# First expert rows asked for inside the attention block, and two batches routed earlier

## The reference, cut to what matters

```python
x = x + _L0_xattn_ref(_layernorm(x, axis=-1), ctx_2048, ctx_2048, ...)   # 16 heads of 8 per batch
x = x + _L0_ffn_ref(_layernorm(x, axis=-1), gate_w, w13, w2)             # 64 experts, 8 chosen per token
# _L0_ffn_ref
logits = jnp.einsum('th,eh->te', x, gate_w)
topk_w, topk_idx = jax.lax.top_k(jax.nn.softmax(logits, axis=-1), 8)
h = jax.nn.silu(x @ w13_e[:128].T) * (x @ w13_e[128:].T)                 # for each expert e
out += c[:, None] * (h @ w2_e.T)
```

## Time and profile before

| | |
|---|---|
| median of 3 executions | 681.9 us |
| the profiled execution's own time | 680.48 us |
| its span, first to last instruction | 678.0 us |
| attention block | 64.6 to 262.7 us |
| first expert stage (held_phase) | 270.9 to about 420 us |
| busy: PE, DVE, ACT, POOL | 481.2, 362.2, 260.7, 368.8 us |
| mean granted TensorE clock | 0.839 |

### The profile page before, as it was taken

One profiled execution on the slowest core, in us unless ns is written; L12 is line 12 of the kernel. 1 busy time (PEld: TensorE's weight loads), 2 busy tenths in 40 slices (PEclk: granted clock), 3 DMA queues, 4 the chain that ended last, 5 costly groups with the idle time before them and its releaser, 6 DMA issues.

```text
span 678.0 us, 12350 instructions
## 1 busy us (share of the span) xinstructions
PE 481.2 (71%) x3519; PEld 368.3 (54%) x3520; DVE 362.2 (53%) x1105; ACT 260.7 (38%) x621; POOL 368.8 (54%) x517
## 2 busy tenths in 40 slices
PE   2641898788888430699989996176674599999960
PEld 1530344344443210588878874165453599999950
DVE  6981675799985560145444443565744144444426
ACT  0351065566668210333323331133342355555520
POOL 9494311116666673156555556226666787777730
PEclk9785597899989655699999999566886699999985
DMA  5089989856579696789999733959922333333327
GB/s 187 0 204 232 338 308 281 236 105 186 169 248 281 205 406 280 218 250 329 327 311 323 264 118 111 390 217 338 401 74 88 94 106 103 106 97 95 128 63 288
DMA packets 78131, 144.15 MB, mean 213 GB/s; under 512 B 12639, under 2 KB 56687, under 8 KB 76289
## 3 DMA queue, kind: packets, MB, share of 16 engines
q1 hardware_dynamic: 52048, 86.41, 39.5%
q0 software_dynamic: 13968, 32.29, 13.0%
q10 hardware_dynamic: 12064, 24.84, 12.5%
HBM read 85.14 MB, written 66.78 MB: 224 GB/s over the span
## 4 chain that ended last, share of the span: by engine, by line
PE 33%; DMA 12%; DVE 5%; POOL 5%; issue 2%; ACT 1%; SPq 1%; POOLq 0%; DVEq 0%
PE sc_ps L1814 11%; DMA hd_side<-held 6%; PE hd_ps_up L1252 6%; PE sc_ps L1796 5%; DMA rows<-hd_side_out,hd_side_target 3%; PE hd_ps_out L1258 2%; DMA sc_rows<-rows 2%; PE hd_ps_x L1230 2%; PE sc_ps L1804 1%; POOL sc_n_root L1494 1%; PE sc_ps L1749 1%; PE sc_ps L1761 1%; POOL sc_n_full L1492 1%; POOL listed L688 1%; PE sc_ps L618 1%
## 5 line engine op out<-in xcount | busy, mean ns | idle before, releaser
L1027 DVE TENSOR_REDUCE at_top<-at_ps_top 128x2 f32<-128x512 f32 x128 | 83.0, 685 | 42.9 <-PE at_ps_top L932 41.8
L1399 POOL DMA_INDIRECT rows<-hd_out,hd_rows x64 | 62.2, 972 | 57.4 <-DVE hd_out L1350 37.6
L1099 ACT ACTIVATE at_prob<-at_ps_score 128x512 f32<-128x512 f32 x128 | 72.3, 594 | 47.8 <-PE at_ps_score L950 47.4
L1252 PE MATMUL hd_ps_up<-hd_x_turned,e_arena 128*128 128x160 f32 x512 | 82.9, 306 | 0.0
L1814 PEld LDWEIGHTS sc_ps<-sc_t_turned,sc_up_w 128*112 128x112 f32 x672 | 81.2, 181 | 2.6
L1814 PE MATMUL sc_ps<-sc_t_turned,sc_up_w 128*112 128x128 f32 x672 | 82.4, 277 | 0.0
L932 PE MATMUL at_ps_top<-e_arena 96*128 96x256 bf16 x256 | 55.4, 304 | 37.0 <-PEq L107 21.9
L1252 PEld LDWEIGHTS hd_ps_up<-hd_x_turned,e_arena 128*128 128x128 f32 x512 | 76.4, 193 | 8.7 <-issue 6.2
L688 POOL DMA_INDIRECT held<-e_extended,e_address x64 | 62.3, 973 | 25.4 <-issue 17.7
L1387 DVE TENSOR_TENSOR hd_inner<-hd_silu,hd_ps_up 128x160 f32<-128x160 f32 x64 | 20.6, 322 | 83.4 <-ACT hd_silu L1337 83.4
L1709 POOL DMA_INDIRECT listed<-sc_empty,sc_index x48 | 46.7, 974 | 14.6 <-issue 12.8
(11 more groups left out here) (267 smaller groups left out, 941.1 us busy)
## 6 DMA issues: line engine op xcount, KB each, us to landing
e_arena<-in_weights SPq DMA_DIRECT2D x52, 384.0 KB, 11.3
held<-e_empty ACTq DMA_DIRECT2D x16, 960.0 KB, 6.3
hd_rows<-held SPq DMA_DIRECT2D x15, 768.0 KB, 9.9
e_w<-in_weights SPq DMA_DIRECT2D x16, 704.0 KB, 10.1
sc_rows<-rows SPq DMA_DIRECT2D x8, 1024.0 KB, 7.3
sc_tile_rows<-listed SPq DMA_DIRECT2D x42, 144.0 KB, 2.2
parts<-op_parts SPq DMA_DIRECT2D x8, 576.0 KB, 6.4
e_arena<-in_weights ACTq DMA_DIRECT2D x12, 384.0 KB, 4.2
```

The source lines that it names most:

```text
L1027: nc.vector.reduce_max(top[:, 2 * h:2 * h + 2], ps_top[at % TOPS][:], AX_X).then_inc(top_found, 1)
L1099: nc.scalar.activation(prob[at % RING][:], ps_score[at % SCORES][:], ACT.Exp, scale=scale).then_inc(prob_ready, 1)
L1252: op = nc.tensor.matmul(ps_up[e % 2][:, part, :], w[:, k, part * P:(part + 1) * P], x_turned[g % 2][:, j, k, :], start=k == 0, stop=k == 1)
L1399: nc.gpsimd.indirect_dma_start(rows_out, to, out_ap, None, bounds_check=TOKENS * LAYER0.chosen - 1, oob_is_err=False).then_inc(semaphore, 16)
```

## The change: what it does

Two buffers, rows0 and side0, which stood in held_phase as the first of its two rings, are allocated in Held, outside the attention's space, together with the five semaphores of their first loads. The five loads of group 0 are issued at the end of attend_phase's SP list, behind a wait for `scattered`; held_phase's SP list begins with group 1. The routing table gets a set of offsets for batch 4, and another for batch 5: all pieces from norm or turn on come up to 8 steps earlier. Batch 3's scatters are again split into four and four, 8 steps apart, so that its last four alternate with the first of batch 4 (in the order 3.4, 4.0, 3.5, 4.1, 3.6, 4.2, 3.7, 4.3, batch and number). merge(5) waits for rank_read too.

```diff
 class Held:
+        self.rows0 = s.sbuf("rows0", [P, EACH, ROW0], F32)
+        self.side0 = s.sbuf("side0", [P, ROW0], F32)
+        self.first_loaded = [s.sem(f"first_loaded{j}") for j in range(EACH)]
+        self.side0_loaded = s.sem("side0_loaded")
+
+    def load_first_rows(self, sp):
+        sp.wait_ge(self.scattered, 16 * LAYER0.chosen * B)
+        for j in range(EACH):
+            if j == 1:
+                sp.dma_start(self.side0[:], self.of_expert[0:EACH, P * ROW0:].rearrange("e (r n) -> e r n", n=ROW0))\
+                    .then_inc(self.side0_loaded, 16)
+            sp.dma_start(self.rows0[:, j, :], self.of_expert[j, 0:P * ROW0].rearrange("(r n) -> r n", n=ROW0)).then_inc(self.first_loaded[j], 16)
...
 class RoutingSteps:
-    LAST_BUT_TWO = dict(AMID, turn=45, keep=46, score=49, choose=49, expo=50, targets=50, rank=50, places=51, weights=51, scatter=53)
+    LAST_BUT_THREE = dict(AMID, turn=45, keep=46, score=49, choose=49, expo=51, rank=51, places=52, targets=53, weights=54, scatter=54)
+    LAST_BUT_TWO = dict(AMID, norm=40, turn=43, keep=44, score=47, choose=47, expo=48, rank=48, places=49, targets=49, weights=50, scatter=51)
...
-        of_batch = [self.AMID] * (B - 3) + [self.LAST_BUT_TWO] + [self.LAST_TWO] * 2
+        of_batch = [self.AMID] * (B - 4) + [self.LAST_BUT_THREE, self.LAST_BUT_TWO] + [self.LAST_TWO] * 2
...
-            apart = H // 2 if first < B * H - H - 4 else LAYER0.chosen // 2
+            apart = H // 2 if b < B - 4 else LAYER0.chosen // 2
...
 attend_phase, sync:
                 ring.load(sp, e)
+            held.load_first_rows(sp)
...
 attend_phase, tensor:
-                if b >= B - 2:
+                if b >= B - 3:
                     pe.wait_ge(routing.rank_read, b)
...
-                    if b + 1 < B - 2:
+                    if b + 1 < B - 3:
                         pe.wait_ge(x_ready, b + 2)
...
 held_phase:
-        rows = [s.sbuf(f"rows{n}", [P, EACH, ROW0], F32) for n in range(RING)]
-        side = [s.sbuf(f"side{n}", [P, ROW0], F32) for n in range(RING)]
+        rows = [held.rows0] + [s.sbuf(f"rows{n}", [P, EACH, ROW0], F32) for n in range(1, RING)]
+        side = [held.side0] + [s.sbuf(f"side{n}", [P, ROW0], F32) for n in range(1, RING)]
...
-            sp.wait_ge(held.scattered, 16 * LAYER0.chosen * B)
-            for g in range(RING):
+            for g in range(1, RING):
                 load_rows(g)
```

More of the change, by code:

```diff
@@ L1141, in held_phase @@
         rows_loaded = [s.sem(f"rows_loaded{n}") for n in range(RING)]
-        first_loaded = [s.sem(f"first_loaded{j}") for j in range(EACH)]
-        side_loaded = [s.sem(f"side_loaded{n}") for n in range(RING)]
+        first_loaded = held.first_loaded
+        side_loaded = [held.side0_loaded] + [s.sem(f"side_loaded{n}") for n in range(1, RING)]
         stored = [s.sem(f"stored{n}") for n in range(OUTS)]
@@ L1175, in load_rows @@
                 n = g % RING
-                if g == 0:
-                    for j in range(EACH):
-                        if j == 1:
-                            sp.dma_start(side[n][:], of_expert[0:EACH, P:HELD, :]).then_inc(side_loaded[n], 16)
-                        sp.dma_start(rows[n][:, j, :], of_expert[j, 0:P, :]).then_inc(first_loaded[j], 16)
-                    return
                 sp.dma_start(rows[n][:], of_expert[EACH * g:EACH * (g + 1), 0:P, :].rearrange("e p n -> p e n"))\
```

## The result

| | kernel before | changed kernel |
|---|---|---|
| median, us (15 runs each, in turn on one chip) | 681.49 | 677.17 |
| ratio, 95% interval | 1 | 0.9937 (0.9911 to 0.9962) |
| the profiled execution: time, span, us | 680.48, 678.0 | 675.59, 673.1 |

The change makes the kernel 4.3 us faster (681.49 - 677.17), by the interval 2.6 to 6.1. The forecast was 675.8 inside 672.8 to 681.2.

What follows compares the result with a forecast made beforehand. The chain of waits was taken to count from PE's start in the expert stage, held back by POOL's scatters and the block's end. Routing 2.0 plus early loads 4.1, 6.1 us, took the median of 681.9 to 675.8, range 672.8 to 681.2.

Steps and rivals of the forecast that it cites:

- Batch 4's steps: Attention's routing: batch 4's weights at 215.55 instead of 221.34, scatter 4.0 at 216.7, with waits at merge(5) and norm(5).
- POOL's end: End of attention: POOL's 35 scatters from 216.7 end at 260.7 instead of 262.66, 2.0 us sooner.
- The tightest batch: Attention's routing: batch 7 wanted at 250.85, ready at 249.5 to 250.3, so no wait, by half a microsecond.
- Group 0's loads: End of attention: `scattered` full 4.0 us after POOL's last scatter, side tile issued at 265.2, landing 5.94 us later at 271.1.
- The block's end: Attention's end: SP there at 267.3, POOL at 267.1, new block 1.9 us on at 269.2.
- The rival that put the price behind the last arrival: Block's end: POOL's 6.4 us begin once SP has come; PE gains 0.7 us, time 681.2; chance 0.14.
- that of the stretched issues: Block's end: SP's five loads meet full queues, take 7.5 us, PE starts 4.3 us later, time 686.2; chance 0.08.
- PE's start: Start of the expert stage: PE starts at 271.15 instead of 277.30, 6.1 us sooner, released by the side tile.
- Group 1 and on: Expert stage: group 1's loads go at 269.2, slack falls from 3.3 to 1.3 us and holds; ring moves as a whole.
- the rival: Expert stage: transfers set the ring's pace or group 1 is late, 3 us of 6.1 return, time 678.8; chance 0.10.
- The sum: Whole kernel: routing 2.0 and group 0 asked for early 4.1, 6.1 us in all, giving 675.8.

Runs made afterwards that it cites:

- side in four: Changed kernel with group 0's four row loads issued by ACT and its side tile by SP as four loads of 32 rows; ratio to kernel before 0.9925.
- rows on ACT: Changed kernel with SP asking for group 0's side tile alone and ACT for its four row tiles; ratio to kernel before 0.9941.
- Batch 3 earlier too: Changed kernel with batch 3's steps also moved earlier and its first four scatters six heads earlier; ratio to kernel before 0.9919.
- 15 copies behind the last: Changed kernel with 15 small unread copies on POOL behind its last scatter, ahead of the block's end; ratio to kernel before 0.9948.
- 28 copies, first run: Changed kernel with 28 small unread copies on POOL ahead of scatter 4.0; ratio to kernel before 0.9945, repeated 1.0004.
- the buffers alone: Kernel before with only group 0's two buffers and five semaphores moved to Held, loads still in the expert block; ratio to kernel before 1.0009.

## Why the prediction was right, by its own steps

*Batch 4's steps.* Foretold: 4.0 at 216.7, 5.8 us sooner. In distances from the cut it went from 15.96 (222.47 - 206.51) to 10.09 (218.22 - 208.13): 5.9 sooner. The wait ahead of it is 0.66 us and not about 1.5, since 3.0 itself came later (3.10 us after the cut and not 2.58): ACT's weights of batch 3 hold it for 1.03 us. The waits at merge(5) and norm(5) are there.

*POOL's end.* Foretold 2.0 us sooner; the pair of traces gives 1.7, the means over four and six traces 1.4, pairs of like clock 1.1 to 1.6, the time 1.5 (0.2 to 2.9). So this term was too large by 0.3 to 0.9 us. The sum took one pair of landmarks where the distance varies from run to run by more than the term. Most of the variation goes with the clock, though side in four has a short stretch (54.82) at 0.86. In the first 20 us behind the cut the mean granted clock was 1.00 of full (2.4 GHz) in the changed kernel's trace and 0.84, a mix of its two levels, in that of rows on ACT:

```profile
208.10:228.10 20.00, 15.55 (x160) 7.22 (x160) 10.19 (x40) 14.36 (x34) 14.41 (x20) 1.00 0.78 252
```

```profile
208.60:228.60 20.00, 17.09 (x146) 7.66 (x144) 7.62 (x33) 13.61 (x32) 13.40 (x19) 0.84 0.78 244
```

*The tightest batch.* Foretold: batch 7 ready half a microsecond ahead of its scatter. In the trace of the changed kernel its weights end at 250.39, 42.26 us from the cut, and it is sent at 44.27. In that with the slower clock its address is ready at 45.1, and POOL waits:

```profile
254.14 0.95 POOL L701 DMA_INDIRECT held<-e_extended,e_address  x1 [0.45 <-DVE e_address L693]
```

So this step held by 2 us at full clock and failed by 0.45 us below it. Batch 3 earlier too shows it as the next bound even at full clock.

*Group 0's loads.* The landing 3.95 us behind the last scatter (266.54 - 262.59) was foretold as 4.0, and SP issues 0.02 us after it and not 0.16. I had argued that the late weights in the queue cost at most 0.5 us. They do not delay the side load, as the trace showed; that they delay the last scatter's landing, by 2.3 us, I had taken into the 4.0 without seeing it. The side tile took 5.41 us for 5.94.

*The block's end.* Foretold: POOL 6.4 us behind its last scatter, SP 6.6, then 1.9. Measured: SP 6.43 (269.02 - 262.59), then 1.58, and 8.01 in all. The rival that put the price behind the last arrival would have had 8.27 behind SP's fifth issue; it is refuted by 1.58 here. That of the stretched issues is refuted too: five in 2.46 us. The DRAIN records show the race: with no loads of SP's ahead of it POOL arrives 6.45 to 6.88 us after its last scatter (three traces), and SP, with its five issues, 6.60 after it. In the five traces with all five issues on SP and no copies POOL's record ends 0.01 to 0.02 us behind SP's, so close that it may end by SP's arrival and not by POOL's own work: SP is last or level with POOL. It costs next to nothing either way, since the block begins 7.68 to 8.06 us behind the last scatter in these five and 7.83 to 8.27 in the three without the issues. Where the weights run on longest (rows on ACT, side in four) POOL needs 7.41 and 7.50, where they have landed 5.3. From the end of POOL's record to the new block it is 1.38 to 1.40 us and not 1.9, and in the trace of the kernel before POOL took 6.88 and not 6.4: the prediction had the sum from the trace (8.27) and the split wrong by half a microsecond, which did no harm here.

*PE's start.* Foretold 6.1 us sooner. From the cut it is 64.25 us (272.38 - 208.13) where it was 70.79 (277.30 - 206.51): 6.5. The margin behind it is thin: PE could have run from about 271.56 (block at 270.60 and 0.96), 0.8 us ahead of the side tile.

*Group 1 and on.* No wait of PE for group 1 in the changed kernel's trace, and the expert stage kept its length there. With the block 3 us late (15 copies behind the last) the chain does run through group 1's side load (278.30 for 8.27 us), so the slack was real and about as small as foretold. In two more traces PE waits for group 1, 0.74 us (28 copies, first run) and 0.29 (side in four). And the stage did not keep its length in every trace: from PE's start to the `sc_rows` load it is 146.8 to 147.3 us in the three traces that ask late and 146.8 to 150.8 in the eleven that ask early, 148.2 on the mean. A microsecond given back there isn't shown, with so few late traces, but it isn't excluded either; the rival had put it at 3.

*The sum.* 6.1 us foretold; the means of both measurements are 4.3 and 6.2 under the kernel before, by the two ratios together 5.0, and against the buffers alone it is 5.8 (4.1 to 7.6). The early ask is 4.2 of it (foretold 4.1), the routing 1.5 (foretold 2.0). In the traces the early ask brings more than foretold (4.4 to 4.9 us from POOL's last scatter to PE's start), above all since the side tile took 5.4 and not 5.94 us, and the routing less: that PE's start came out so near is in part two misses that cancel. Between that start, 6.5 us sooner, and the 5.0 in the time lie the scatter between runs and perhaps the microsecond in the expert stage; the record doesn't tell them apart.

## What to carry to other kernels

A load at the head of a new block pays the old block's end even when its data has long landed; asking for it as the last piece of the old block, into a buffer that both blocks own, takes that price off the path, but only until the new block's own start becomes the bound, which here would have let PE start only 0.8 us sooner. Before such an edit, write down for each engine when it arrives at the block's end: an issue that is put on an engine that would not have come last costs nothing there (SP's five left the new block where it was, since POOL needed as long). How much one more would cost on the engine that does come last, no run here shows. And where a stage is bound by a string of equal pieces on one engine, moving the pieces forward pays only down to the readiness of the last one, which should be read at the slowest clock that traces show and not in one profile.

## What the runs showed of the hardware

- POOL's time at a block's end after indirect DMAs is serial work behind its last instruction, not a wait since the last scatter: its DRAIN record begins behind 3.82 us of copies and still takes 5.30 us, as long as POOL needs behind its last scatter without them (5.30 to 5.31, three traces). With weights still being loaded it is 6.45 to 7.50 (the five such traces in which POOL came last).
- An indirect DMA's landing depends on who shares the engines: 1.64 us after POOL is done with it on an idle hardware queue, in each of three traces, and 3.4 to 4.9 us while weights are being loaded.
- Once POOL's DRAIN record has ended, barriers and two clearings took 1.38 to 1.40 us in each of 14 traces.
- One kernel measured twice with 12 runs each gave ratios of 0.9945 and 1.0004; half a per cent is about what one such comparison can tell here.
